# First norms of a decoder block with a state-space layer, taken batch by batch beside the projections, and in part inside the recurrence

## The chip, the cores and the metric

One core of one Trainium2 chip. The time is the device time of one execution in microseconds (us); the time before is the median of 3 runs. TensorE (PE) multiplies matrices, VectorE (DVE), ScalarE (ACT) and GpSimd (POOL) work on tiles of 128 partitions, and SyncE (SP) issues all the DMAs. Each has its own queue, worked off in order; semaphores tie them together.

## The reference, cut to what matters

Four sequences (batches) of 512 positions with 512 features. What the change touches is the front of the first of three layers:

```python
x = x + _L0_attn_ref(_layernorm(x, axis=-1), ...)
# _layernorm: (x - m) / sqrt(v + 1e-5) over the features
# _L0_attn_ref:
res = hidden_states
h = _rmsnorm(hidden_states, rms1_w)       # x * rsqrt(mean(x*x) + 1e-5) * w
h = res + _mamba(h, ...)
# _mamba:
zxbcdt = x @ in_proj_w.T                   # 2688 outputs: z, x, B, C, dt
dt = softplus(dt_in @ dt_proj_w.T + dt_proj_b)
# for each position: h = exp(dt * A) * h + dt * x * B;  y = C * h, summed over 16 states
y = (y + D_skip * x_full) * silu(z)
```

Behind it stand the out projection, an MLP, a quantised attention and an MLP with 4-bit weights; the change leaves them as they are.

## The kernel before

**Layout.** Features lie on the partitions in 4 tiles of 128 (`FT = 4`), positions on the free axis: one batch is 4 x 512 columns, 1 MB. Sums over features are matmuls with a matrix of 1/512 (`mean_w`), whose result is the mean in every partition. The matmuls with data are split: each float is a high part (fp32r) and a low part, and `three_pass` makes three matmuls out of one (high x high, high x low, low x high).

**Norms (on VectorE L1164 to L1201).** All four batches go through each step before the next step begins: x is loaded whole into `xin`; TensorE forms the means (`mean_of`), `centre` subtracts them, ScalarE squares (`norm_squares`), TensorE averages the squares (`squares_mean`), ScalarE takes the root, `rstd` on VectorE the reciprocal, and VectorE writes the normed x into `res`, which SP stores to HBM as `res_d` for use long after. The second norm does the same again with the squares of `res` (`rms_scale`, `split_hi`, `split_lo`), and leaves the high and low parts `xhi` and `xlo`. A barrier of all five engines follows (`phase_end(..., 1)`).

**Lead-in and recurrence.** The loop `for g in range(-2, STEPS)` stands on every engine. A step `g` is one block of 128 of the 1024 channels of one batch (`STEPS = 32`, 8 steps to a batch) and has 16 turns `c`, one for each state. In each turn TensorE spreads a row of dt and one of v over the partitions (`spread_dt`, `spread_v`), ScalarE forms the decay, VectorE multiplies v with B (`make_drive`) and scans along the positions (`scan`), GpSimd multiplies with C (`read_out`), and TensorE gathers (`gather_four`). The rings hold 3 drives, 6 states and 8 read-outs. Steps -2 and -1 are the lead-in: they have no scans and only do the jobs that the first steps need.

A *job* is one of 21 tiles of 128 outputs of the in projection for one batch (`project`), three jobs a step, two steps ahead. Job 0 is dt, 1 is the first tile of x, 2 of B, 3 of C. For batch 0 each needs its weights first: load (`load_wraw`, two buffers), high part on ScalarE (`w_high`), low part on VectorE (`w_low`), and a store of both to `w_d`, from where the other batches load them. ScalarE takes a job's result out of PSUM (`take`), SP spills it to HBM (`spill`), with 4 copies for x and B, and loads it back in the layout that the scan needs (`load_x`, `load_b`, `load_c`). `soft_*` make dt out of job 0, `dt_x` multiplies it with x to v, and `load_pack` copies the high and low halves of dt and v into packs that TensorE spreads from.

**What sets the order.** All orders are written out by hand. SP's queue is in one order too: a load waits behind every wait ahead of it.

## Time and profile before

| | us |
|---|---|
| median of 3 runs | 2953.04 (2950.15 to 2955.85) |
| the profiled execution, its time | 2957.49 |
| its span, first to last instruction | 2955.6 |
| busy: TensorE, VectorE, ScalarE, GpSimd | 2665.8, 2147.2, 1157.1, 1217.0 |
| first scan starts, last scan starts | 146.0, 1108.0 |
| granted TensorE clock, mean over the span | 0.931 |

The profile is of one execution. An instruction's busy time is its own; two neighbours on an engine can overlap a little. Where an engine idles, the profile names what released it. The granted clock is a share of 2.4 GHz: 0.5 is 1.2 GHz. A matmul in plain f32 shows as two rows, each with its own weight load.

### The profile page before, as it was taken

What the parts mean: (1) busy time and instruction counts of PE and PEld (TensorE: products, weight loads), DVE (VectorE), ACT (ScalarE), POOL (GpSimd) and SP (SyncE); (2) the same over time, 40 slices, a digit from 0 to 9 for tenths busy, and PEclk for the clock granted to TensorE, in tenths of its full rate; (3) what the DMA queues carried; (4) which work ended last, traced back from release to release, by engine and by line L of the source; (5) the groups of instructions that cost most, each with busy time, mean ns of one, the idle gap of its engine ahead of it and who ended that gap; (6) DMA issues with size and microseconds to landing.
All of it is one profiled execution on the core that took longest, in us unless ns stands there. A gap on an engine that the chain in (4) does not pass through costs nothing.

```text
span 2955.6 us, 32384 instructions
## 1 busy us (share of the span) xinstructions
PE 2665.8 (90%) x11120; PEld 1892.8 (64%) x11128; DVE 2147.2 (73%) x2711; ACT 1157.1 (39%) x1665; POOL 1217.0 (41%) x816
## 2 busy tenths in 40 slices
PE   6388898889888885699999999999989999999999
PEld 2244344444344424588888877887877788888887
DVE  5499999999999994544346667776867875555553
ACT  3355555555555543432225444343333332222221
POOL 0088898889888870101000104222412422222221
PEclk9699898889899867899999999999999999999999
DMA  3455465464556316412121111212111111111111
GB/s 139 157 170 160 133 178 157 110 201 137 135 164 173 109 50 246 135 44 78 43 72 43 62 39 41 66 43 60 48 42 38 47 46 50 51 48 45 51 50 65
DMA packets 152212, 275.34 MB, mean 93 GB/s; under 512 B 27248, under 2 KB 27760, under 8 KB 151536
## 3 DMA queue, kind: packets, MB, share of 16 engines
q1 hardware_dynamic: 152048, 273.27, 31.1%
q8 instruction: 88, 1.44, 0.2%
q14 instruction: 76, 0.62, 0.1%
HBM read 178.27 MB, written 61.34 MB: 81 GB/s over the span
## 4 chain that ended last, share of the span: by engine, by line
PE 71%; DVE 10%; ACT 8%; issue 5%; POOL 3%; DMA 2%; SPq 1%; DVEq 0%; POOLq 0%; ACTq 0%
PE ps L1596 19%; PE ps L1597 18%; PE ps L1598 18%; PE ps L1636 8%; ACT ps L791 5%; PE ps L1646 4%; DVE state L1255 4%; POOL read L1058 2%; DVE rs L1172 1%; PE ps L1574 1%; DMA vpack<-vl 1%; PE ps L1763 1%; PE ps L1737 1%; PE ps L1707 1%; DMA owraw<-in_out_w 0%
## 5 line engine op out<-in xcount | busy, mean ns | idle before, releaser
L1058 POOL TENSOR_TENSOR read<-state,c_t 128x512 f32<-128x512 f32 x512 | 655.5, 1293 | 142.2 <-DVE state L1255 116.7
L1255 DVE TENSOR_TENSOR_SCAN state<-ps,drive 128x512 f32<-128x512 f32 x512 | 618.4, 1208 | 13.5 <-ACT ps L791 12.4
L1596 PE MATMUL ps<-xh,ghi 128*128 128x512 f32 x1536 | 607.9, 396 | 0.8 <-issue 0.8
L1598 PE MATMUL ps<-xh,glo 128*128 128x512 f32 x1536 | 598.8, 390 | 0.0
L1597 PE MATMUL ps<-xl,ghi 128*128 128x512 f32 x1536 | 598.5, 390 | 0.0
L1105 POOL TENSOR_TENSOR wdeq<-packed,scales 128x1024 f32<-128x1024 f16 x96 | 260.3, 2712 | 798.6 <-DVE packed L1374 798.6
L791 ACT ACTIVATE ps<-ps,a_exp 128x512 f32<-128x512 f32 x512 | 338.9, 662 | 469.0 <-PE ps L1636 467.7
L1541 DVE TENSOR_TENSOR act_o<-act_o,ps 128x512 f32<-128x512 f32 x192 | 131.7, 686 | 313.1 <-PE ps L1598 298.2
L1246 DVE TENSOR_TENSOR drive<-ps,b_t 128x512 f32<-128x512 f32 x512 | 339.8, 664 | 22.6 <-PE ps L1636 22.2
L1636 PE MATMUL ps<-dpack,sel 128*128 128x512 f32 x512 | 260.5, 509 | 104.4 <-DVE state L1255 103.4
L996 ACT ACTIVATE ahi<-act_o 128x512 fp32r<-128x512 f32 x192 | 121.5, 633 | 560.8 <-DVE act_o L1541 560.8
L1596 PEld LDWEIGHTS ps<-xh,ghi 128*128 128x128 f32 x1536 | 288.7, 188 | 63.6 <-issue 4.3
L1597 PEld LDWEIGHTS ps<-xl,ghi 128*128 128x128 f32 x1536 | 288.8, 188 | 61.8 <-issue 3.1
L1598 PEld LDWEIGHTS ps<-xh,glo 128*128 128x128 f32 x1536 | 288.7, 188 | 60.4
L1596 PE MATMUL ps<-ahi,ghi 128*128 128x512 f32 x768 | 306.3, 399 | 20.2 <-issue 20.2
L1597 PE MATMUL ps<-alo,ghi 128*128 128x512 f32 x768 | 300.8, 392 | 0.0
L1598 PE MATMUL ps<-ahi,glo 128*128 128x512 f32 x768 | 300.7, 392 | 0.0
L1636 PE MATMUL ps<-vpack,sel 128*128 128x512 f32 x512 | 251.8, 492 | 36.9 <-DMA vpack<-vl 23.6
L1527 DVE TENSOR_TENSOR res<-res,ps 128x512 f32<-128x512 f32 x192 | 130.8, 685 | 193.0 <-PE ps L1598 190.9
L1636 PEld LDWEIGHTS ps<-dpack,sel 128*128 128x128 f32 x512 | 108.1, 211 | 231.5 <-DVE state L1255 222.0
L1636 PEld LDWEIGHTS ps<-vpack,sel 128*128 128x128 f32 x512 | 106.1, 207 | 229.3 <-issue 97.9
L858 ACT ACTIVATE ghi<-wdeq 128x1024 fp32r<-128x1024 f32 x96 | 100.9, 1051 | 298.1 <-POOL wdeq L1105 266.4
(177 smaller groups left out, 3792.9 us busy)
## 6 DMA issues: line engine op xcount, KB each, us to landing
whi<-w_d SPq DMA_DIRECT2D x63, 256.0 KB, 3.9
wlo<-w_d SPq DMA_DIRECT2D x63, 256.0 KB, 4.8
x_d<-ev SPq DMA_DIRECT2D x32, 256.0 KB, 3.3
x_t<-x_d SPq DMA_DIRECT2D x32, 256.0 KB, 4.8
b_d<-ev SPq DMA_DIRECT2D x32, 256.0 KB
b_t<-b_d SPq DMA_DIRECT2D x32, 256.0 KB, 4.1
c_d<-ev SPq DMA_DIRECT2D x32, 256.0 KB, 3.0
c_t<-c_d SPq DMA_DIRECT2D x32, 256.0 KB, 3.2
```

The lines of the kernel that those rows point to most:

```text
L791: act.activation(ps[:, n % 2, :], ps[:, n % 2, :], ACT.Exp, scale=a_exp[:, col:col + 1]).then_inc(decay_ready, 1)
L996: act.activation(ahi[n // 2][:, cols(n % 2)], act_o[n % 2][:, :], ACT.Copy)\
L1058: pool.tensor_tensor(read[:, n % RRING, :], state[:, n % SRING, :], c_t[:, g % 2, :], ALU.mult).then_inc(read_ready, 1)
L1105: pool.tensor_tensor(wdeq[:, :].rearrange("p (h n) -> p h n", h=2), codes, scale, ALU.mult).then_inc(deq, 1)
L1246: dve.tensor_tensor(drive[:, n % DRING, :], ps[:, 2 + n % 2, :], b_t[:, g % 2, :], ALU.mult).then_inc(drive_ready, 1)
L1255: dve.tensor_tensor_scan(state[:, n % SRING, :], ps[:, n % 2, :], drive[:, n % DRING, :], 0.0, ALU.mult, ALU.add)\
L1527: dve.tensor_tensor(res[:, f, cols(b)], res[:, f, cols(b)], ps[:, free_bank(24 * E + 16 + k), :], ALU.add).then_inc(added, 1)
L1541: dve.tensor_tensor(act_o[n % 2][:, :], act_o[n % 2][:, :], ps[:, free_bank(24 * E + 2 * n + 1), :], ALU.mult)\
L1596: pe.matmul(out_, w_h, x_h, start=(start and k == 0), stop=False)
L1597: pe.matmul(out_, w_h, x_l, start=False, stop=False)
L1598: last = pe.matmul(out_, w_l, x_h, start=False, stop=(stop and k == n - 1))
L1636: pe.matmul(ps[:, bank, :], sel[:, 4 * (j % 2) + m, :], pack[j // 2][:, :], start=True, stop=True).then_inc(done, 1)
```

## The change

- The norms are formed per batch (`column_mean`, `centre`, `squares`, `variance`, one instruction for each of the 4 tiles), in place in `xlr[b]` and `xhr[b]`. Reciprocal roots are two ScalarE instructions, `Ln` and `Exp` with scale -0.5 (`root_1`, `root_2`), so the reciprocals on VectorE go. The mean square of the second norm is worked out from the first (`hat_variance`: variance times the first reciprocal root, twice) and not by squares and matmuls, and `both_roots` multiplies the two reciprocal roots.
- The normed x that is stored to `res_d` (`normalise`) is made by GpSimd: of batches 0 and 1 in the lead-in, of 2 and 3 in steps 2 and 4.
- `scale_x`, `split_hi` and `split_lo` of batch 0 stand in front of its first projection; those of batches 1, 2 and 3 stand in the recurrence, in steps 2 and 3, 10 and 11, 18 and 19.
- The barrier behind the norms goes, and so do two of ScalarE's table loads. The lead-in is written out by hand on each engine in place of steps -2 and -1. The means and variances of batches 1 to 3 stand in it, between the projections.
- Loads of x come batch by batch; batch 0 comes as 4 loads, and the weights of the first two jobs come right behind it.
- `copy_x0` copies the first x tile for step 0 within SBUF instead of through HBM; `load_pack` is cut in two, and for step 0 the packs are loaded ahead of other work. C's tiles 1 and 2 are jobs 4 and 5 (`C_TILES`).

The diff, cut to its core:

```diff
@@ SP
+            for f in range(FT):
+                sp.dma_start(xlr[0][:, f, :], t["x"][:, f, cols(0)]).then_inc(x0_loaded[f], 16)
...
             store_w(0)
             store_w(1)
-            for g in range(-2, STEPS):
+            store_hat(0)
+            store_w(2)
+            copy_x0()
+            load_pack_dt(0)
+            spill(B0)
+            spill(X0)
+            load_pack_v(0)
+            load_b(0)
+            store_w(3)
...
+            for g in range(STEPS):
...
+                if g == 1:
+                    store_hat(1)
+                if g in (4, 6):
+                    store_hat(g // 2)
@@ ACT
+            def root_1(b):
...
+                act.activation(r1, ps[:, VAR_BANK[b], :], ACT.Ln, bias=eps_col[:, 0:1]).then_inc(ln_log, 1)
+                act.wait_ge(ln_log, 2 * b + 1)
+                act.activation(r1, r1, ACT.Exp, scale=-0.5).then_inc(ln_r1, 1)
...
+            squares(0)
+            w_high(0)
+            w_high(1)
+            root_1(0)
...
+            root_2(2)
+            squares(3)
+            take(4)
+            root_1(3)
+            w_high(6)
+            root_2(3)
+            take(5)
+            w_high(7)
...
+                    for b in (1, 2, 3):
+                        if g == CT * b - 5 and c % 4 == 1:
+                            split_hi(b, c // 4)
@@ POOL
+            def normalise(b, f):
+                r1, u = ln_rows[b]
+                pool.wait_ge(ln_r1, b + 1)
+                pool.tensor_tensor(hat(b)[:, f, :], xlr[b][:, f, :], r1, ALU.mult).then_inc(ln_hat, 1)
...
+                    if g in (2, 4) and c % 4 == 3:
+                        normalise(1 + g // 2, c // 4)
@@ DVE
-            def rstd(use, b):
-                dve.wait_ge(root_ready, B * use + b + 1)
-                dve.reciprocal(rs[:, cols(b)], rs[:, cols(b)]).then_inc(rstd_ready, 1)
-                dve.wait_ge(rstd_ready, B * use + b + 1)
...
+                    for b in (1, 2, 3):
+                        if g == CT * b - 6 and c % 4 == 1:
+                            scale_x(b, c // 4)
+                        if g == CT * b - 5 and c % 4 == 2:
+                            split_lo(b, c // 4)
@@ PE
+            pe.wait_ge(mean_loaded, 16)
+            column_mean(0)
+            variance(0)
+            column_mean(1)
+            project_whole(0)
+            project_whole(1)
+            pe.wait_ge(dwlo_ready, 1)
+            dt_project(0)
+            variance(1)
+            project_whole(2)
+            column_mean(2)
+            project_whole(3)
+            dt_project(1)
+            variance(2)
+            column_mean(3)
+            project_whole(4)
+            variance(3)
+            project_whole(5)
```

**The order on TensorE, in front of the first projection.** Rows with `mean_w` are means and mean squares, rows with `whi` or `wlo` the projection. Before, it ended with batch after batch of squares and the barrier:

```order
L1574 MATMUL ps<-sq,mean_w 128x512 x3
L1574 MATMUL ps<-sq,mean_w 128x512 [waits squared]
L1574 MATMUL ps<-sq,mean_w 128x512 x3
L1596 MATMUL ps<-xhi,whi_67 128x512 [waits dwlo_ready,wlo_ready,sel_ready,phase_done]
L1597 MATMUL ps<-xlo,whi_67 128x512
L1598 MATMUL ps<-xhi,wlo_70 128x512
L1596 MATMUL ps<-xhi,whi_67 128x512
```

And now, where batch 0 stands in front of it, and one mean of batch 1:

```order
L1689 MATMUL ps<-xlr_62,mean_w 128x512 [waits x0_loaded3]
L1698 MATMUL ps<-xhr_58,mean_w 128x512 [waits ln_squared] x4
L1689 MATMUL ps<-xlr_63,mean_w 128x512 [waits x_loaded1]
L1689 MATMUL ps<-xlr_63,mean_w 128x512 x3
L1706 MATMUL ps<-xh_50,whi_78 128x512 [waits ln_lo,wlo_ready]
L1707 MATMUL ps<-xl_54,whi_78 128x512
L1708 MATMUL ps<-xh_50,wlo_81 128x512
```

The first projection moved from behind 48 such matmuls and the barrier to behind 12.

**The order on TensorE at the end of the lead-in** (rows with `sel` are the spreads of the recurrence). Before:

```order
L1598 MATMUL ps<-dthi,dwlo 128x512
L1596 MATMUL ps<-xhi,whi_69 128x512
L1597 MATMUL ps<-xlo,whi_69 128x512
L1598 MATMUL ps<-xhi,wlo_72 128x512
L1636 MATMUL ps<-vpack_89,sel 128x512 [waits pack_loaded0]
L1636 MATMUL ps<-vpack_89,sel 128x512
L1636 MATMUL ps<-dpack_85,sel 128x512
```

And now:

```order
L1707 MATMUL ps<-xl_54,whi_79 128x512
L1708 MATMUL ps<-xh_50,wlo_82 128x512
L1698 MATMUL ps<-xhr_61,mean_w 128x512 [waits ln_squared] x4
L1706 MATMUL ps<-xh_50,whi_80 128x512 [waits job_taken,wlo_ready]
L1707 MATMUL ps<-xl_54,whi_80 128x512
...
L1708 MATMUL ps<-xh_50,wlo_83 128x512
L1745 MATMUL ps<-vpack_102,sel 128x512 [waits ln_u,pack_loaded0,ln_centred,sel_ready]
L1745 MATMUL ps<-vpack_102,sel 128x512
L1745 MATMUL ps<-dpack_98,sel 128x512
```

The variance of batch 3 (L1698) now stands between jobs 4 and 5, job 5 is done before the first spread, and that spread waits for the norms' last use of its banks too.

**The order on VectorE in step 2 of the recurrence** (`state` rows are scans, `drive` rows the products in front of them). Before:

```order
L1246 TENSOR_TENSOR drive<-ps,b_t 128x512 [waits scan_done,vb_ready]
L1255 SCALAR_TENSOR_TENSOR state<-ps,drive 128x512 [waits read_ready,decay_ready,drive_ready]
L1246 TENSOR_TENSOR drive<-ps,b_t 128x512 [waits scan_done,vb_ready]
L1255 SCALAR_TENSOR_TENSOR state<-ps,drive 128x512 [waits read_ready,decay_ready,drive_ready]
L1211 TENSOR_TENSOR wlo_72<-wraw,whi_69 128x512 [waits whi_ready]
L1246 TENSOR_TENSOR drive<-ps,b_t 128x512 [waits scan_done,vb_ready]
L1255 SCALAR_TENSOR_TENSOR state<-ps,drive 128x512 [waits read_ready,decay_ready,drive_ready]
```

And now:

```order
L1315 TENSOR_TENSOR drive<-ps,b_t 128x512 [waits scan_done,vb_ready]
L1324 SCALAR_TENSOR_TENSOR state<-ps,drive 128x512 [waits read_ready,decay_ready,drive_ready]
L1279 SCALAR_TENSOR_TENSOR xlr_63<-xlr_63,rms_71,dwraw 128x512 [waits ln_hat,ln_r12]
L1315 TENSOR_TENSOR drive<-ps,b_t 128x512 [waits scan_done,vb_ready]
L1324 SCALAR_TENSOR_TENSOR state<-ps,drive 128x512 [waits read_ready,decay_ready,drive_ready]
L1315 TENSOR_TENSOR drive<-ps,b_t 128x512 [waits scan_done,vb_ready]
L1324 SCALAR_TENSOR_TENSOR state<-ps,drive 128x512 [waits read_ready,decay_ready,drive_ready]
L1290 TENSOR_TENSOR wlo_83<-wraw,whi_80 128x512 [waits whi_ready]
```

A scaling (L1279) stands between a scan and the next drive, four times in this step; in step 3 a low part (L1285) does, and the same for the other two batches in steps 10 and 11, 18 and 19.

## Rows read from the trace of the kernel before

**Rows 1.** Busy us (xcount) by stretch; then clock, DMA share, GB/s.

```profile
0.00:99.00 99.00, 48.06 (x96) 19.80 (x96) 68.02 (x44) 34.03 (x28) 0.20 (x4) 0.81 0.29 103
99.00:146.00 47.00, 26.09 (x84) 20.10 (x85) 8.88 (x11) 15.44 (x26) 6.81 (x5) 0.72 0.73 235
146.00:1108.00 962.00, 833.54 (x3060) 421.60 (x3060) 933.53 (x1100) 501.16 (x814) 841.82 (x665) 0.87 0.51 145
```

**Rows 2.** Scan and drive: ns shortest, median, longest; first and last start.

```profile
L1255 DVE TENSOR_TENSOR_SCAN state<-ps,drive x512: 1200/1207/1224, 146.0 to 1108.0; 128x512 f32<-128x512 f32 x171
...
L1246 DVE TENSOR_TENSOR drive<-ps,b_t x512: 652/661/695, 144.8 to 1106.3; 128x512 f32<-128x512 f32 x171
```

**Rows 3.** Waits on VectorE, 146 to 1108 us: us, times, longest.

```profile
DVE drive L1246 <- PE ps L1636: 14.6, 24, 0.7
DVE state L1255 <- ACT ps L791: 12.4, 31, 0.5
```

**Rows 4.** Groups of instructions, 0 to 99 us: busy us, mean ns, idle before.

```profile
L1172 DVE RECIPROCAL rs<-rs 128x512 f32<-128x512 f32 x8 | 26.8, 3348 | 11.3 <-ACT rs L695 11.2
...
L1186 DVE SCALAR_TENSOR_TENSOR xin<-res,rms,rs 128x512 f32<-128x512 f32 x16 | 11.0, 747 | 0.1
...
L1177 DVE TENSOR_TENSOR xlo<-xin,xhi 128x2048 fp32r<-128x2048 f32 x4 | 9.1, 2286 | 0.0
...
L695 ACT ACTIVATE rs<-ps,eps_col 128x512 f32<-128x512 f32 x8 | 5.0, 684 | 5.5 <-PE ps L1574 5.5
L1211 DVE TENSOR_TENSOR wlo<-wraw,whi 128x512 fp32r<-128x512 f32 x2 | 1.3, 682 | 0.0
```

**Rows 5.** DMA issues, 0 to 4.5 us: KB each, median us to landing.

```profile
xin<-in_x SPq DMA_DIRECT2D x1, 1024.0 KB, 5.9
mean_w<-in_mean_w SPq DMA_DIRECT2D x1, 64.0 KB, 1.8
```

**Rows 6.** Timeline of TensorE, the norms: start us, us.

```profile
26.00 13.90 PE L1574 MATMUL ps<-sq,mean_w 128*128 128x512 f32 x32
44.74 5.40 PE L1574 MATMUL ps<-sq,mean_w 128*128 128x512 f32 x8 [4.85 <-ACT sq L688]
```

**Rows 7.** Timeline of the lead-in.

```profile
114.69 0.64 ACT L762 ACTIVATE sp_exp<-sp_abs 128x512 f32<-128x512 f32 x1
...
115.90 0.62 ACT L775 ACTIVATE sp_log<-sp_exp 128x512 f32<-128x512 f32 x1
116.00 0.69 DVE L1235 SCALAR_TENSOR_TENSOR sp_rest<-ps,sp_exp 128x512 f32<-128x512 f32 x1 [4.97 <-ACT ps L769]
...
117.07 1.63 DVE L1211 TENSOR_TENSOR wlo<-wraw,whi 128x512 fp32r<-128x512 f32 x1 [0.38 <-ACT whi L720]
...
143.51 0.50 PEld L1636 LDWEIGHTS ps<-vpack,sel 128*128 128x128 f32 x2 [16.45 <-DMA vpack<-vl]
```

**Rows 8.** Groups of instructions, 148 to 1300 us.

```profile
L1058 POOL TENSOR_TENSOR read<-state,c_t 128x512 f32<-128x512 f32 x512 | 655.5, 1293 | 142.2 <-DVE state L1255 116.7 <-PE ps L1646 20.4 <-issue 0.5
...
L1211 DVE TENSOR_TENSOR wlo<-wraw,whi 128x512 fp32r<-128x512 f32 x13 | 12.9, 994 | 0.0
```

**Rows 9.** TensorE by stretch: busy us, clock, DMA share, GB/s.

```profile
71.00:99.00 28.00, 0.00 (x0) 0.50 0.00 0
99.00:103.00 4.00, 3.98 (x9) 0.50 0.44 143
...
113.30:119.20 5.90, 5.90 (x27) 0.99 0.71 242
```

**Rows 10.** DMA issues, 99 to 150 us.

```profile
wraw<-in_in_w SPq DMA_DIRECT2D x8, 256.0 KB, 3.9
...
vpack<-vh SPq DMA_DIRECT2D x2, 128.0 KB, 3.9
```

**Rows 11.** The chain that ended last, in the lead-in: start us, us.

```profile
120.03 6.79 DMA b_d<-ev
```

More of the change, by code:

```diff
@@ L79, in build @@
     res = place("res", [P, FT, T], F32, 0)
-    xhi = place("xhi", [P, FT, T], F32R, after())
-    xlo = place("xlo", [P, FT, T], F32R, after())
-    SCAN0 = 32768
-    FREE0 = after()
+    XH0, XL0, FREE0 = 32768, 65536, 98304
+    xh = [place(f"xh{b}", [P, FT, S], F32R, XH0 + 8192 * b) for b in range(B)]
+    xl = [place(f"xl{b}", [P, FT, S], F32R, XL0 + 8192 * b) for b in range(B)]
+    xhr = [place(f"xhr{b}", [P, FT, S], F32, XH0 + 8192 * b) for b in range(B)]
+    xlr = [place(f"xlr{b}", [P, FT, S], F32, XL0 + 8192 * b) for b in range(B)]
     mean_w = place("mean_w", [P, P], F32, (top - base - 3072) // 32 * 32)
@@ L95, in build @@
     round_col = place("round_col", [P, 1], F32, after())
[L98 to L101 removed]
+    NORM_END = FREE0 + 57344
     wraw = place("wraw", [P, 2, FT, P], F32, NORM_END)
@@ L118, in build @@
     dt_t = place("dt_t", [P, S], F32, after())
+    row_r = place("row_r", [P, S], F32, after())
+    row_u = place("row_u", [P, S], F32, after())
     assert after() <= top - base - 3072
@@ L703, in _, with table @@
[L703 to L712 removed]
+            def table(number):
+                act.add_instruction(mybir.InstLoadActFuncSet(
+                    name=nc.get_next_instruction_name(), act_func_set_id=number, ins=[], outs=[]))
@@ L792, in decay, with soften @@
                                scale=a_exp[:, col:col + 1]).then_inc(decay_ready, 1)
+            def soften(q):
+                soft_abs(q)
+                soft_pos(q)
+                soft_exp(q)
+                soft_one(q)
+                soft_log(q)
+            act.wait_ge(consts_ready, 2)
+            table(EXP_LN_SET)
+            squares(0)
+            w_high(0)
+            w_high(1)
+            root_1(0)
+            act.wait_ge(dw_loaded, 16)
+            act.activation(dwhi[:, :], dwraw[:, :], ACT.Copy).then_inc(dwhi_ready, 1)
+            root_2(0)
+            act.wait_ge(loaded_consts, 16 * 6)
+            act.activation(a_exp[:, :], a_log[:, :], ACT.Exp).then_inc(a_ready, 1)
+            for f in range(FT):
+                split_hi(0, f)
+            w_high(2)
+            take(0)
+            squares(1)
+            take(1)
+            soften(0)
+            root_1(1)
+            take(2)
+            w_high(3)
+            dt_high(0)
+            root_2(1)
+            squares(2)
+            v_high(0)
+            w_high(4)
+            take(3)
+            soften(1)
+            root_1(2)
+            w_high(5)
+            root_2(2)
[6 more added lines that the diff above has]
+            w_high(7)
             act.wait_ge(a_ready, 2)
-            act.add_instruction(mybir.InstLoadActFuncSet(
-                name=nc.get_next_instruction_name(), act_func_set_id=EXP_LN_SET, ins=[], outs=[]))
-            for g in range(-2, STEPS):
+            for g in range(STEPS):
                 nb, k, jobs = step_jobs(g)
@@ L1268, in skip_y @@
                                          op0=ALU.mult, op1=ALU.add).then_inc(y_ready, 1)
-            for g in range(-2, STEPS):
+            centre(0)
+            w_low(0)
+            w_low(1)
+            hat_variance(0)
+            dve.wait_ge(dwhi_ready, 1)
+            dve.tensor_tensor(dwlo[:, :], dwraw[:, :], dwhi[:, :].bitcast(F32), ALU.subtract)\
+               .then_inc(dwlo_ready, 1)
+            both_roots(0)
+            dve.wait_ge(loaded_consts, 16 * 6)
+            for f in range(FT + 1):
+                if f < FT:
+                    scale_x(0, f)
+                if f:
+                    split_lo(0, f - 1)
@@ L1271, in _ @@
+            hat_variance(2)
+            w_low(5)
+            centre(3)
+            both_roots(2)
+            hat_variance(3)
+            w_low(6)
+            both_roots(3)
+            w_low(7)
+            dve.tensor_copy(ident16[:, :], ident[:, :]).then_inc(consts_ready, 1)
+            make_drive(0, 0)
+            for g in range(STEPS):
                 nb, k, jobs = step_jobs(g)
                 first = IN_TILES * nb + 3 * k
-                if g == 0:
-                    make_drive(0, 0)
```

371 lines of the change are left out of this document (195 added, 176 removed).

## The prediction, made before the changed kernel was run

> **What bounds the kernel now.** I read the views in this order. First the busy time by stretch [rows 1]: the span falls into a stretch of norms (0 to 99 us), a lead-in (99 to 146), the recurrence (146 to 1108), a gap, and the part behind it, which the change does not touch. In the norms VectorE is busy 68 of 99 us and GpSimd 0.2; TensorE works 48 us of them and the last 28 not at all. In the recurrence VectorE is busy 934 of 962 us. Second, the two instructions that make up the recurrence [rows 2]: 512 scans of 1.21 us and 512 drives of 0.66 us, which is nearly all of the 934. The first scan starts at 146.0 and the last at 1108.0. Third, VectorE's waits in that stretch [rows 3]: 27.0 us in all, none over 0.7. So the recurrence is bound by VectorE, in its own order, and two numbers decide what the change is worth: when the first scan starts, and how much work VectorE does between the first scan and the last.
>
> **What is removed.** The eight reciprocals (26.8 us), the 16 scalings (11.0 us), the batch-wide low parts (9.1 us) and two more batch-wide passes of that length, centring and normalising, all on VectorE [rows 4], stand one behind another in front of the barrier. With them go a second pass of squares on ScalarE and its 16 mean matmuls. The barrier lets the first projection start at 99.0.
>
> **What comes before the first scan now.** Four terms.
>
> (a) *Batch 0 to its first projection.* The first of four 256 KB tiles is issued at about 0.7; before, a 1 MB load took 5.9 us and a 64 KB one 1.8 us [rows 5], so TensorE starts near 4 and is not starved afterwards. A mean or variance block is four matmuls, eight rows in the trace: 13.9 us for 32 of them, so 3.4 us a block at full clock, and 5.4 us for a block begun after idling [rows 6]. Mean ends near 9.7. The first tile's centring (0.6) and square (0.6) run ahead of the rest, so variance ends near 14.5. The two roots need Ln, Exp, two VectorE products, Ln, Exp, one product: with 0.69 us for ScalarE from PSUM [rows 4], 0.61 to 0.64 for Ln and Exp and 0.69 for a dependent VectorE row [rows 7], 4.6 us, and 5.1 with the hand-offs, to 19.7. Eight tile operations on VectorE (four scalings, four low parts), 0.6 each when back to back, and one copy on ScalarE follow: 25.2, and three more passes end projection 0 at 26. The four normalisings move to GpSimd, 1.29 us each [rows 8]; the last ends at 21.4 and is used at about 22.
>
> (b) *TensorE's queue from there.* A projection is 12 passes of 0.23 us at full clock, 2.7 us, or of 0.43 at half, 5.1 (27 passes in 5.9 us and 9 in 4.0) [rows 9]. Projection 1 (2.7) runs while ScalarE copies and VectorE centres batch 1 (2.5), takes a low part (0.6) and splits dt (0.6), so the first dt matmuls end at 29.7. Then in its queue: variance 1, projection 2, mean 2, projection 3, dt, variance 2, mean 3, projection 4, variance 3: five blocks at 3.4, three projections at 2.7 and 0.7 make 25.8, so 55.5.
>
> (c) *Waits inside it.* The raw weights come through two buffers, reloaded by SP after the low part has been stored, 3.9 us to landing [rows 10]. The load of tile 5 now stands on SP behind the packs of step 0, behind eight copies of B and X and behind the load of B, which waits for the copies to land; in the old chain that landing took 6.8 us [rows 11]. ScalarE copies tile 5 before it squares batch 3, so variance 3 is late by it: I take 5 us.
>
> (d) *After variance 3.* Two roots (5.1), the eighth weight tile on ScalarE and VectorE (1.3), two drives (1.3): the first scan at 55.5 + 5 + 7.7 = 68 at full clock. Projection 5 (2.7) and the first spreads lie beside the roots. The packs, loaded 3.9 us after the last half is issued [rows 10], are there by about 51, since SP now issues them ahead of most spills; before, TensorE waited for them until 143.5 [rows 7].
>
> TensorE's clock is the open term. In the old lead-in the granted clock was 0.72 [rows 1]; it was at 1.2 GHz from 99 to 103, after idling, and at 2.4 GHz from 113.3 to 119.2, in a dense run [rows 9]. The new queue is denser than the old one but has waits. At half clock throughout, every block takes 6.8 us and every projection 5.1: (a) and projection 1 end at 38 instead of 29.7, variance 1 to projection 5 are five blocks, four projections and dt once, 34 + 20.5 + 1.3 = 56, and the last step takes some 4: the first scan at 98. I take 5 us more than at full clock, as if 5 us of the work ran at half pace: the **first scan at 73**, between 66 and 98. That is 73 us before the old 146.
>
> The Trainium skill, "TensorE: Matmul & The Clock Gate", Part 1, says that the default state is the throttled one and activity releases it. The row from 71 to 99, idle at 0.50 [rows 9], agrees; the page would not change the sum, only make the half-clock case likelier if waits of (c) are longer than taken.
>
> **What is added to the recurrence.** Batches 1 to 3 are scaled and split there: 12 scalings and 12 low parts on VectorE, all with both inputs in SBUF. The nearest row is the weights' low part, of the same shape, with GpSimd at work beside it: 0.99 us mean of 13 in the recurrence against 0.68 in the norms [rows 4, 8], and once 1.63 [rows 7]. VectorE has no room, so each adds its length less the 0.07 by which neighbours overlap: 24 x 0.92 = **22 us**, between 24 x 0.58 = 14 and 24 x 1.56 = 37. They do not wait: hats and roots of each batch are a step or more older. ScalarE gets 12 copies of 0.6, with 461 of 962 us free; no cost. GpSimd gets eight normalisings, 10.3 us, in steps 2 and 4. A step is 16 read-outs and 5 others, 27 us of its time in about 32 that such a step takes VectorE; 5.2 more makes 32. Six state buffers cover a lag, so nothing, at most 2 us a step. SP stores 1 MB of hats at steps 1, 4 and 6; DMA is busy 0.51 there [rows 1] and the next step's loads have a step of slack: nothing. If that cover went, three times 3 us. TensorE loses nothing; its projections read other tiles of the same size.
>
> By a rule of the Trainium skill the price would be higher. "SBUF — State Buffer", § Who interferes with whom, says that VectorE with two SBUF inputs and GpSimd reading SBUF exclude each other for a whole instruction. Here an addition could wait out a read-out of 1.29 us: 24 x (0.68 + 1.29 - 0.07) = 45 us instead of 22. The 13 low parts, at 0.99 on average, say that most of the wait does not fall on VectorE, and I keep 22; the 45 is a rival below.
>
> **Sum.** 73 saved, 22 given back: 51 us. The profiled execution took 2957.5 (span 2955.6); 2957.5 - 51 = 2906.5. It stood 4.45 above the median of 2953.04, so against the median **2902**.
>
> **Rivals.**
>
> *Clock and waits (17%).* TensorE stays mostly at half clock, or waits on each hand-off; the first scan is at 98. For it: the 0.72. Against: full clock in every dense stretch. 2953 - 48 + 22 = 2927.
>
> *All overlaps (12%).* First scan at 67, and the additions cost 14 or fill some of the 27.0 us of VectorE's waits: 2953 - 79 + 14 = 2888.
>
> *Whole-instruction exclusion (7%).* As worked out from the two lengths: 2953 - 73 + 45 = 2925.
>
> *The norms of batch 0 don't start the work sooner (2%).* All first loads share one queue. If the tile that projection 2 needs lands only after some 6 MB are in, about 20 us later than taken, the first scan is at 93: 2922. Against: the loads before drained by 21, and the first weight copies here stand ahead of 3 MB of x.
>
> *Lock-step (2%), the other side.* The place is TensorE's in-order queue: each mean and variance of batches 1 to 3 stands in front of a projection and waits for centring and squares. If nothing overlaps, a batch costs mean 6.8, centring 2.5, square 0.6, variance 6.8 and roots 5.1, 22 us, and the lead-in keeps its 47: 26 + 47 + 66 = 139. With the additions at 37 us: 2953 - 7 + 37 = 2983. It decides once the first scan is later than 146 - 22 = 124. Against it: the order puts a projection or a block of another batch between nearly all links.
>
> **How the numbers follow.** My forecast, 2902, has 60%; its own terms give 2890 to 2915. A measurement of this kernel can tell about 0.2%, 6 us, from no change. Four cases of five lie more than 6 us below 2953, and only lock-step is above; with it, and a little for its milder forms, faster is 97%, same 1%, slower 2%. The range 2884 to 2928 takes in the clock, overlap and exclusion cases at their centres and leaves out their tails and lock-step.
>
> **What would show it.** The first projection near 22 and the first scan near 73 (66 to 98); granted clock in the stretch from 20 to 73 above 0.8; TensorE there busy well over half; the distance from first to last scan 962 + 22 = 984, with scalings and low parts in it at 0.9 to 1.0 us; the 1847.6 us from the start of the last scan to the end of the span unchanged. The forecast is wrong if the first scan is later than 98, if the additions exceed 1.6 us each, or if steps 2 and 4 grow by more than their own VectorE work, which would be GpSimd.

## The result, and the profile after

| | before | after |
|---|---|---|
| median, measured together (4 runs each) | 2953.70 us | 2904.87 us (2903.83 to 2910.90) |
| ratio | | 0.984, 95% interval 0.9828 to 0.9852 |
| the profiled execution, its time and span | 2957.49, 2955.6 | 2910.90, 2909.1 |
| first scan, last scan | 146.0, 1108.0 | 78.4, 1059.7 |
| from first to last scan | 962.0 | 981.3 |
| from the start of the last scan to the end of the span | 1847.6 | 1849.4 |
| granted TensorE clock, mean | 0.931 | 0.939 |

The kernel is 1.6% faster; 2902 was predicted, with a range of 2884 to 2928. In the profiled execution, the first scan comes 67.6 us earlier, the distance to the last is 19.3 us longer and the part behind 1.8 longer: 67.6 - 19.3 - 1.8 = 46.5, which is the difference of the two spans.

The busy time by stretch, which answers to [rows 1] (columns: TensorE, its weight loads, VectorE, ScalarE, GpSimd, then clock, DMA share and GB/s):

```profile
0.00:26.00 26.00, 13.94 (x26) 5.76 (x27) 13.27 (x17) 9.90 (x16) 7.02 (x8) 0.93 0.91 314
26.00:74.00 48.00, 39.35 (x119) 24.01 (x118) 22.29 (x34) 26.73 (x46) 12.29 (x9) 0.86 0.55 175
74.00:1056.00 982.00, 837.25 (x3056) 419.91 (x3054) 955.42 (x1126) 508.29 (x828) 858.79 (x671) 0.87 0.51 147
```

Norms and lead-in are now one stretch in which TensorE is busy 53 of 74 us. Taken exactly from the first scan to the last, VectorE is busy 955.6 of 981.3 us, against 933.5 of 962.0 before: 22.1 us more work and 2.8 us less idle time make the 19.3 by which the distance grew. GpSimd went from 842 to 861.

The scan, as in [rows 2], and VectorE's waits from the first scan on, as in [rows 3]:

```profile
L1324 DVE TENSOR_TENSOR_SCAN state<-ps,drive x512: 1198/1216/1231, 78.4 to 1059.7; 128x512 f32<-128x512 f32 x171
```

```profile
DVE state L1324 <- ACT ps L827: 11.6, 27, 0.8
DVE drive L1315 <- PE ps L1745: 11.2, 18, 0.7
```

The waits of these two lines fell by 4.2 us (27.0 to 22.8), all idle time together by 2.8, so the work that was added took little of them. Its own price, in the groups of instructions from 90 to 1060 us (busy us, mean ns):

```profile
L1290 DVE TENSOR_TENSOR wlo<-wraw,whi 128x512 fp32r<-128x512 f32 x12 | 12.0, 1000 | 0.0
L1285 DVE TENSOR_TENSOR xl<-xlr,xh 128x512 fp32r<-128x512 f32 x12 | 11.9, 991 | 0.0
L1279 DVE SCALAR_TENSOR_TENSOR xlr<-xlr,rms,selraw 128x512 f32<-128x512 f32 x4 | 4.4, 1104 | 0.0
L1279 DVE SCALAR_TENSOR_TENSOR xlr<-xlr,rms,row_u 128x512 f32<-128x512 f32 x4 | 4.1, 1028 | 0.0
L1279 DVE SCALAR_TENSOR_TENSOR xlr<-xlr,rms,dwraw 128x512 f32<-128x512 f32 x4 | 3.4, 862 | 0.0
```

The low parts of the weights stayed where they had been (994 ns in [rows 8], 1000 now), and the low parts of x cost the same. The 24 added instructions are busy 23.8 us. Less 0.07 each where neighbours overlap that makes 22.1. How much of the distance they cost is known to about 4 us only, since a distance is read from one execution: it grew by 19.3 against the kernel before (962.0), but the run with Ln and Exp alone, further down, has the same recurrence as the kernel before and a distance of 958.2, from which it would be 23.1.

TensorE's timeline in front of the first scan (start us, us, then in brackets the idle time before and what ended it):

```profile
3.68 6.18 PE L1689 MATMUL ps<-xlr,mean_w 128*128 128x512 f32 x8 [3.68 <-DMA mean_w<-in_mean_w]
11.30 3.70 PE L1698 MATMUL ps<-xhr,mean_w 128*128 128x512 f32 x8 [1.44 <-ACT xhr L730]
14.84 3.60 PE L1689 MATMUL ps<-xlr,mean_w 128*128 128x512 f32 x8
25.37 0.77 PE L1706 MATMUL ps<-xh,whi 128*128 128x512 f32 x1 [6.93 <-DVE xl L1285]
...
33.41 3.60 PE L1698 MATMUL ps<-xhr,mean_w 128*128 128x512 f32 x8
...
55.83 0.39 PE L1708 MATMUL ps<-xh,wlo 128*128 128x512 f32 x1
64.87 6.30 PE L1698 MATMUL ps<-xhr,mean_w 128*128 128x512 f32 x8 [8.65 <-ACT xhr L730]
```

There are two holes, 6.93 us in front of the first projection and 8.65 us in front of batch 3's variance, and the block behind the second takes 6.30 us instead of 3.60. The granted clock was 0.98 in the hole from 57 to 60, 0.50 from 61.5 to 64.8, 0.58 over this block and 1.00 behind it. The chain that ended last shows what the second hole is (start us, us, what):

```profile
42.96 0.46 SPq L523
...
43.46 1.72 SPq L524
...
45.23 0.71 SPq L502
...
50.14 1.75 SPq L502
...
51.93 0.51 SPq L502
...
52.48 1.09 SPq L502
...
57.53 0.43 SPq L470
...
58.00 4.17 DMA wraw<-in_in_w
...
62.20 0.64 ACT whi L761
...
62.86 0.69 DVE wlo L1290
63.55 0.61 DVE xlr L1259
...
64.19 0.64 ACT xhr L730
...
64.87 6.32 PE ps L1698 x8
```

`L502` is the line that spills B and X: eight copies, between 45.23 and 53.57, that SyncE issues one after another at about 1 us each. The store of weight tile 3, with which the load of tile 5 is issued, stands behind them. From 42.96 to 58.00 this chain is SyncE's issuing alone, 14.3 us without a wait; of the 21.9 us up to the start of the variance no other engine or transfer has as much.

### The profile page after: what moved, and what is told of

Same layout as the page of the kernel before. It is cut to its first block, busy times and chain, and to the rows that moved or that the text cites. A ratio compares the mean times of both kernels' runs of the same rounds, so it can differ in the third digit from the quotient of the medians.

```text
span 2909.1 us, 32439 instructions
## 1 busy us (share of the span) xinstructions
PE 2651.7 (91%) x11096; PEld 1882.2 (65%) x11096; DVE 2135.0 (73%) x2735; ACT 1153.9 (40%) x1690; POOL 1247.4 (43%) x832
## 4 chain that ended last, share of the span: by engine, by line
PE 72%; DVE 10%; ACT 8%; issue 4%; POOL 3%; DMA 1%; SPq 1%; DVEq 0%; POOLq 0%; ACTq 0%
PE ps L1706 19%; PE ps L1707 19%; PE ps L1708 19%; PE ps L1745 8%; DVE state L1324 5%; ACT ps L827 5%; PE ps L1757 5%; POOL read L1140 2%; PE ps L1897 1%; PE ps L1871 1%; PE ps L1841 1%; DMA vpack<-vl 0%; DVE drive L1315 0%; DVE act_o L1650 0%; DMA owraw<-in_out_w 0%
## 5 line engine op out<-in xcount | busy, mean ns | idle before, releaser
L1140 POOL TENSOR_TENSOR read<-state,c_t 128x512 f32<-128x512 f32 x512 | 665.3, 1311 | 144.9 <-DVE state L1324 126.7
L1324 DVE TENSOR_TENSOR_SCAN state<-ps,drive 128x512 f32<-128x512 f32 x512 | 622.8, 1217 | 13.8 <-ACT ps L827 11.6
L1315 DVE TENSOR_TENSOR drive<-ps,b_t 128x512 f32<-128x512 f32 x512 | 344.4, 673 | 11.9 <-PE ps L1745 11.2
```

What stands on the lines that cost most here:

```text
L1140: pool.tensor_tensor(read[:, n % RRING, :], state[:, n % SRING, :], c_t[:, g % 2, :], ALU.mult).then_inc(read_ready, 1)
L1315: dve.tensor_tensor(drive[:, n % DRING, :], ps[:, 2 + n % 2, :], b_t[:, g % 2, :], ALU.mult).then_inc(drive_ready, 1)
L1324: dve.tensor_tensor_scan(state[:, n % SRING, :], ps[:, n % 2, :], drive[:, n % DRING, :], 0.0, ALU.mult, ALU.add)\
```

## The experiments

All stand against the kernel before, measured with them (its medians 2954.22 to 2955.03; 2953.70 beside the change). "First scan" and "distance" are of the profiled execution, and distances of kernels with the same recurrence differ by up to 2 us among the changed ones and by 3.8 between the kernel before and that with Ln and Exp. The intervals of neighbours in this table overlap; where a difference of 4 or 5 us is called one below, the single executions of the two kernels don't overlap. The changed kernel's own profile was its slowest execution; in three experiments that leave the lead-in's critical path alone (24 more products, scalings early, late turns), the first scan stood at 76.7, 76.8 and 77.5, so 77 is its usual place.

| kernel | median us | ratio (95%) | first scan | distance |
|---|---|---|---|---|
| change | 2904.87 | 0.9828 to 0.9852 | 78.4 | 981.3 |
| load of tile 5 first | 2900.96 | 0.9800 to 0.9832 | 72.4 | 981.8 |
| filler | 2905.13 | 0.9817 to 0.9848 | 75.6 | 980.0 |
| norms first | 2932.25 | 0.9908 to 0.9941 | 103.4 | 981.0 |
| before, with Ln and Exp | 2937.86 | 0.9925 to 0.9955 | 128.7 | 958.2 |
| 24 more products | 2918.26 | 0.9862 to 0.9895 | 76.7 | 992.9 |
| late turns | 2907.18 | 0.9824 to 0.9853 | 77.5 | 981.8 |
| scalings early | 2899.75 | 0.9795 to 0.9831 | 76.8 | 976.3 |
| SyncE order 1 | 2901.50 | 0.9804 to 0.9834 | 72.0 | 980.8 |
| SyncE order 2 | 2897.67 | 0.9793 to 0.9820 | 68.9 | 980.1 |
| all together | 2898.13 | 0.9797 to 0.9824 | 67.9 | 978.3 |
| order 2, six scalings in idle time | 2892.51 | 0.9781 to 0.9808 | 68.7 | 973.9 |

In all eleven experiments the stretch behind the last scan was 1844.4 to 1848.7 us. It is unchanged within 4 us, and what moves the time beyond that are the two numbers the prediction had named.

### What the lead-in waits for

**The load of weight tile 5 moved ahead of the copies.**

```diff
             load_pack_dt(0)
+            store_w(3)
             spill(B0)
...
             load_b(0)
-            store_w(3)
```

> Theory: in the changed kernel the first scan (78.4 us) is set by SP's queue: the load of weight tile 5 is issued at 58.0 behind eight copies of B and X, and variance 3 and both roots of batch 3 follow it. Here SP stores tile 3 and loads tile 5 ahead of these copies, all else as it was. Variance 3 should begin near 57 instead of 64.9 and the first scan come 5 to 9 us earlier, 70 to 73; loads of tiles 6 and 7 are late next. Median near 2898. Rival, TensorE's own work sets the lead-in: nothing moves, 78. Rival, the packs and B for step 0 set it: they are issued 1.4 us later here, so the first scan comes later, 79 to 80.

Median 2900.96, 3.9 below the change; the first scan 6.0 earlier in the profile. Its TensorE timeline and its chain of waits:

```profile
56.73 3.70 PE L1698 MATMUL ps<-xhr,mean_w 128*128 128x512 f32 x8
```

```profile
58.38 4.02 DMA c_d<-ev
...
64.20 5.58 DMA wraw<-in_in_w
```

The hole of 8.65 us and the slow block are gone, at one line moved: the cause is shown. Not all of the 11 us between 64.87 + 6.30 and 56.73 + 3.70 reach the first scan, for another thing is late next: the load of tile 7, which stands behind the wait for the spill of C on the same queue. TensorE now has a hole of 5.65 us later, in front of a spread. The first scan came where the theory had it; the median was 3 us above its 2898.

**A filler in the hole**, to tell the wait from the clock: 36 matmuls whose result is not used, which leave the wait as it is.

```diff
             project_whole(4)
+            for k in range(36):
+                pe.matmul(ps[:, 0, :], xh[0][:, 0, 0:P], xh[0][:, 0, :], start=True, stop=True)
             variance(3)
```

> 36 matmuls whose result nobody reads stand between job 4 and variance 3, where TensorE waits 8.7 us and its granted clock falls to 0.50. Theory: the clock stays at full, variance 3 takes 3.4 us instead of 6.3, and the first scan comes 2.9 us earlier, 75.5; median near 2902. Rival, the granted clock isn't what makes variance 3 long or what follows waits for something else: 78.4 as before, or later by what the 36 overrun.

```profile
64.75 3.62 PE L1698 MATMUL ps<-xhr,mean_w 128*128 128x512 f32 x8
```

The block starts where it did, and takes 3.62 us instead of 6.30: behind a hole of 8.65 us TensorE was at 1.2 GHz for most of it (0.58), behind matmuls at 2.4 (1.00). The first scan came 2.8 us earlier in the profile (1.4 against the usual 77), but the median, 2905.13, is the change's, where 2902 had been expected. The clock alone is worth less here than can be told; the hole is what costs.

**The norms of batches 1 to 3 put ahead of the first projection**, to see what the order by itself is worth. Kept are Ln and Exp, the tile-by-tile passes, the missing barrier.

```diff
             pe.wait_ge(mean_loaded, 16)
-            column_mean(0)
-            variance(0)
-            column_mean(1)
+            for b in range(B):
+                column_mean(b)
+                variance(b)
             project_whole(0)
```

(and the same on ScalarE and VectorE.)

> The changed kernel with all means, variances and roots of batches 1 to 3 in front of the first projection instead of between the projections; nothing is removed. Theory: TensorE's six blocks (20.6 us at full clock) and the root chains then delay the first projection from 25.4 to about 46, and the lead-in behind it needs some 40 instead of 53, so the first scan comes at 84 to 92, 6 to 14 us later, median 2911 to 2919: the order between the projections is worth about a third of these norms' cost. Rival, the order is worth their whole cost: the first scan at 100 or later. Rival, SP's queue sets the lead-in so far that it makes no difference: 78 to 80.

Median 2932.25, 27.4 above the change, first scan at 103.4: the theory's 84 to 92 failed, and the rival with 100 or later held. VectorE's timeline:

```profile
31.04 0.69 DVE L1261 TENSOR_TENSOR dwraw<-dwraw,ps 128x512 f32<-128x512 f32 x1 [5.58 <-ACT dwraw L741]
...
41.09 0.69 DVE L1261 TENSOR_TENSOR selraw<-selraw,ps 128x512 f32<-128x512 f32 x1 [4.10 <-ACT selraw L741]
...
51.08 0.69 DVE L1261 TENSOR_TENSOR row_u<-row_r,ps 128x512 f32<-128x512 f32 x1 [4.04 <-ACT row_r L741]
```

The same step of three batches is 10.0 us apart. Mean, centring, square, variance and roots of a batch are one chain through three engines, and with nothing between them nothing fills its gaps. In the change they are filled with projections. This is the lock-step rival in a mild form: 10 us a batch, not 22, since the next batch's mean still lies beside the roots.

**The kernel before, with its eight reciprocals replaced by Ln and Exp.**

```diff
-                    act.activation(rs[:, cols(b)], bank, ACT.Sqrt, bias=eps_col[:, 0:1])\
+                    act.activation(rs[:, cols(b)], bank, ACT.Ln, bias=eps_col[:, 0:1])\
...
+                    act.activation(rs[:, cols(b)], rs[:, cols(b)], ACT.Exp, scale=-0.5)\
...
+            act.add_instruction(mybir.InstLoadActFuncSet(
+                name=nc.get_next_instruction_name(), act_func_set_id=EXP_LN_SET, ins=[], outs=[]))
...
-                dve.reciprocal(rs[:, cols(b)], rs[:, cols(b)]).then_inc(rstd_ready, 1)
```

> The kernel before with one part of the change alone: the eight reciprocal roots are Ln and Exp on ScalarE, the eight reciprocals of 3.35 us on VectorE are gone, everything else stays, the barrier and the batch-wide order too. Theory: VectorE's chain in front of the barrier loses 26.8 us less what ScalarE's second instruction and the next wait give back, so the first scan comes 20 to 27 us earlier than 146, near 123, and the median is near 2930; the order and the barrier are worth the rest of the 68 us. Rival, the reciprocals are the whole of it and the order nothing: 2905. Rival, the squares and mean matmuls take over as the bound: less than 15 us gained.

First scan 17.3 us earlier, median 2937.86, 16.9 below the kernel before: between what the theory (20 to 27) and the rival (less than 15) had said. Two of ScalarE's four table loads up to the lead-in, 1.28 us each, went with the square roots. VectorE's groups from 0 to 82 us, in the two passes that use the roots:

```profile
L1189 DVE SCALAR_TENSOR_TENSOR xin<-res,rms,rs 128x512 f32<-128x512 f32 x16 | 10.9, 748 | 11.6 <-ACT rs L698 11.5
...
L1202 DVE TENSOR_TENSOR res<-xin,rs 128x2048 f32<-128x2048 f32 x4 | 8.9, 2288 | 7.8 <-ACT rs L698 7.8
```

VectorE lost the 26.8 us of [rows 4] and waits 19.3 us for roots instead of 11.2; 26.8 less these 8.1 is 18.7, near the 17.3 by which the first scan moved. Of the 68 us by which the first scan moved, some 17 belong to the roots with their table loads and some 25 to the order; the two were measured from different kernels and need not add up. What the barrier, the missing second pass of squares and the early packs make of the rest was not tried apart.

### What the additions to the recurrence cost

**24 more of them.** Subtractions of the same shape, from SBUF to SBUF, with a result that nobody uses, in steps 12 to 14.

```diff
+                    if g in (12, 13, 14) and c % 2 == 0:
+                        dve.tensor_tensor(flat(wraw[:, 0, :, :]), xh[0][:, 0, :].bitcast(F32),
+                                          xl[0][:, 0, :].bitcast(F32), ALU.subtract)
```

> 24 more subtractions on VectorE of the kind that the change put into the recurrence (128x512, both inputs in SBUF, the result into a buffer nobody reads), in steps 12 to 14. Theory of the prediction, 0.92 us each in a stretch that VectorE fills: the distance from the first to the last scan grows by 22 us, from 981.3 to 1003, and the median to 2927. Rival, VectorE has slack and part of them is free: under 14. Rival, each waits out a whole GpSimd instruction: 45.

The median rose by 13.4 us, the distance by 11.6. The theory's 22 failed, and the number is that of the first rival, under 14; but slack was not the reason. Over the steps in which they stand, from one skip product (`y_t`) to the fifth after it, the time went from 148.5 to 164.1 us, 0.65 us each, which is their busy time, 0.717, less the overlap of 0.07. The other 4 us by which the distance is shorter lie in steps that are the same in both kernels. In the groups of instructions from 455 to 560 us, first of the change, then of this kernel:

```profile
L1140 POOL TENSOR_TENSOR read<-state,c_t 128x512 f32<-128x512 f32 x57 | 72.9, 1290 | 13.0 <-DVE state L1324 12.6
```

```profile
L1140 POOL TENSOR_TENSOR read<-state,c_t 128x512 f32<-128x512 f32 x50 | 72.0, 1450 | 15.4 <-DVE state L1324 15.2
...
L1392 DVE TENSOR_TENSOR wraw<-xh,xl 128x512 f32<-128x512 f32 x24 | 17.2, 717 | 0.0
```

The added instruction took 717 ns, hardly more than alone, and GpSimd's read-outs went from 1290 to 1450 ns. Somebody does wait, but here it is GpSimd, which has time. In the change it is VectorE in part (0.99 us). So what an addition costs is its own length in both cases, and it is the length that differs. What decides which of the two engines waits was not settled; the next run tried one idea.

**The scalings and low parts in turns 10 to 13 of their steps instead of one in every four turns** (and ScalarE's high parts in turns 8 to 11).

```diff
-                        if g == CT * b - 6 and c % 4 == 1:
-                            scale_x(b, c // 4)
-                        if g == CT * b - 5 and c % 4 == 2:
-                            split_lo(b, c // 4)
+                        if g == CT * b - 6 and 10 <= c < 14:
+                            scale_x(b, c - 10)
+                        if g == CT * b - 5 and 10 <= c < 14:
+                            split_lo(b, c - 10)
```

> The scalings and low parts of batches 1 to 3 stand in turns 10 to 13 of their steps, one a turn, instead of in every fourth turn from 1 and 2. Theory: what one costs depends on whether GpSimd reads at that moment; turns 0, 1, 2, 6 and 8 have a second GpSimd instruction, turns 9 to 15 have one and idle time. In turns like that 24 more cost 0.5 us each, here 24 cost 0.84. So the steps with them get shorter by 24 x 0.3 = 4 to 8 us in all, first to last scan near 975, median near 2898. Rival, the place in a step doesn't matter: 981. Rival, four in a row pile up behind GpSimd or the states' ring: longer, 985.

Median 2907.18, distance 981.8: no gain, as the first rival had it. The same groups as above, of this kernel:

```profile
L1290 DVE TENSOR_TENSOR wlo<-wraw,whi 128x512 fp32r<-128x512 f32 x12 | 14.3, 1193 | 0.0
L1285 DVE TENSOR_TENSOR xl<-xlr,xh 128x512 fp32r<-128x512 f32 x12 | 10.7, 893 | 0.0
```

The low parts of x became 98 ns cheaper and the scalings some 150, those of the weights 193 ns dearer; the 36 together are busy 35.1 us instead of 35.8. The place in the step moves most of the wait from one instruction to another and does not remove it.

**The scalings of batches 1 and 2 in the lead-in**, with the normalising of batch 2, which must be first.

```diff
             hat_variance(2)
+            for f in range(FT):
+                scale_x(1, f)
             w_low(5)
...
             both_roots(2)
+            for f in range(FT):
+                scale_x(2, f)
...
-                        if g == CT * b - 6 and c % 4 == 1:
+                        if b == 3 and g == CT * b - 6 and c % 4 == 1:
```

> The scalings of batches 1 and 2 and the hats of batch 2 move from the recurrence into the lead-in, where VectorE stands idle from 54 to 63 and from 66.5 to 72.6 and GpSimd from 53.6 to 79.8. Theory: there they are free, and the distance from first to last scan falls by 8 x 0.9 = 7 us, the first scan stays at 78.4 within 1 us; median near 2898. Rival, the place in the recurrence is as good since VectorE waits there anyway (27 us in all): the distance falls by less than 3 us. Rival, they delay centring 3 or the roots: the first scan comes up to 5 us later.

Median 2899.75, 5.1 below the change; the distance fell by 5.0 where 7 had been expected, the first scan did not move from its usual place. Eight instructions in time that VectorE idled away cost nothing, and 0.63 us each came back.

### Is there a better kernel

**SyncE's queue in another order**, twice. The first put the weight tiles forward, and X and C behind tile 4 and B's load:

```diff
             load_pack_dt(0)
+            store_w(3)
             spill(B0)
-            spill(X0)
             load_pack_v(0)
             load_b(0)
-            store_w(3)
-            spill(3)
             store_w(4)
+            spill(X0)
+            spill(3)
+            store_w(5)
             load_c(0)
             load_x(1)
-            store_w(5)
```

> SP's queue in the lead-in in another order: tile 3 stored and tile 5 loaded ahead of the copies of B, the packs of v and B's load ahead of the copies of X, tiles 4 and 5 stored ahead of the store of C. In the run with tile 5 first alone the first scan came at 72.4 and then waited for tile 7, whose load stood behind the wait for C. Theory: SP's order is the bound and this one frees more of it: first scan at 67 to 69, median 2895. Rival, the copies themselves (8.8 us of issuing) only move, and their late landing holds up tile 4's result or step 1's x: 72 or later.

Median 2901.50, no better than moving tile 5 alone: the rival held. B's load now stands close behind B's copies and waits for them to land, and the X copies, pushed back, land late themselves:

```profile
48.64 7.51 DMA b_d<-ev
...
60.05 4.15 DMA x_d<-ev
```

The second left the X copies behind the B copies and moved weight tile 3 ahead of both, and tiles 4 and 5 ahead of the spill of C:

```diff
             load_pack_dt(0)
+            store_w(3)
             spill(B0)
             spill(X0)
             load_pack_v(0)
             load_b(0)
-            store_w(3)
-            spill(3)
             store_w(4)
+            store_w(5)
+            spill(3)
             load_c(0)
             load_x(1)
-            store_w(5)
```

> SP's queue alone, in a third order: tile 3 stored and tile 5 loaded ahead of the copies of B and X, both sets of copies where they were, then the packs of v and B's load, then tiles 4 and 5 stored (and 6 and 7 loaded) ahead of the store of C and its wait. The run with tile 5 first alone was held up by tile 7 behind the wait for C (72.4), the run with X's copies late by their landing (72.0). Theory: each order shows the next wait on SP, and with both out of the way variance 3, ending near 60, and its roots are next: first scan 67 to 70, median near 2896. Rival: the copies' issuing, 8.8 us, keeps the packs until 61, and the first scan stays at 72.

Median 2897.67, 7.2 below the change; first scan 68.9, as the theory had it.

**All of it together**: order 2, the scalings early, job 5 ahead of batch 3's variance, and batch 3's roots and weight tile 7 moved into step 0.

```diff
             project_whole(4)
-            variance(3)
             project_whole(5)
+            variance(3)
...
             centre(3)
             both_roots(2)
-            hat_variance(3)
+            for f in range(FT):
+                scale_x(1, f)
             w_low(6)
-            both_roots(3)
-            w_low(7)
+            for f in range(FT):
+                scale_x(2, f)
...
+                    if g == 0 and c == 1:
+                        w_low(7)
+                    if g == 0 and c == 4:
+                        hat_variance(3)
+                    if g == 0 and c == 7:
+                        both_roots(3)
```

> The pieces that gained, together: the third SP order; scalings of batches 1 and 2 and hats of batch 2 in the lead-in; project 5 ahead of variance 3; the roots of batch 3 and weight tile 7 in the turns of step 0. Theory: the first scan then waits for the packs, B and the sixth projection only, 64 to 67, and the distance from first to last scan is 981 - 5 for the scalings + 3 for the products and the tile that move in, near 979: median 2886 to 2891, faster than both kernels. Rival: the gains overlap, since the lead-in's idle time that the scalings use is the time that the SP order takes away: the first scan at 70 or later, median 2896 or more.

Median 2898.13, the same as order 2 alone, where 2886 to 2891 had been expected. Its chain:

```profile
58.50 4.15 DMA wraw<-in_in_w
...
62.67 0.64 ACT whi L761
...
64.61 2.07 DVE xlr L1284 x3
...
66.81 1.20 DVE drive L1320 x2
```

The scalings of batch 2 (L1284) stand behind the low part of tile 6, for which VectorE waits, and in front of the first drive: 2.7 us of them are on the path. What had been taken out of the lead-in went to step 0, where VectorE is full: the distance, 978.3, is 2.0 longer than with the scalings early alone.

**Order 2 with six of the eight scalings put where VectorE idles**: four in the 3.5 us in front of batch 3's first products, two in the 1.6 us in front of tile 6's low part; batch 2 is normalised in the lead-in again, and nothing is moved into step 0.

```diff
             both_roots(2)
+            for f in range(FT):
+                scale_x(1, f)
             hat_variance(3)
+            scale_x(2, 0)
+            scale_x(2, 1)
             w_low(6)
             both_roots(3)
```

> SyncE's second order with six of the eight scalings of batches 1 and 2 put into VectorE's idle time of that lead-in (3.5 us in front of batch 3's first products, 1.6 us in front of weight tile 6's low part), the last two of batch 2 left in step 10, and batch 2 normalised behind batch 1 on GpSimd in the lead-in. Theory (an added instruction costs its length wherever VectorE is full and nothing where it idles on the first scan's path): first scan stays near 69, the distance from first to last scan falls from 980.1 by 6 x 0.84 = 5 to 975, median 2893, 4.5 below 2897.7. Rival (the lead-in is as full as it looks after e_best: what is put there delays the first scan by as much): first scan 72 to 74, distance 975, median 2897 to 2898.

Median 2892.51 (2889.76 to 2895.13, none as slow as the fastest of order 2, 2896.89), ratio 0.9795. First scan 68.7, distance 973.9; 69, 975 and 2893 had been expected. Its VectorE timeline:

```profile
59.11 3.75 DVE L1281 SCALAR_TENSOR_TENSOR xlr<-xlr,rms,dwraw 128x512 f32<-128x512 f32 x4
62.78 0.68 DVE L1268 TENSOR_TENSOR row_u<-row_r,ps 128x512 f32<-128x512 f32 x1
63.49 0.69 DVE L1270 TENSOR_TENSOR row_u<-row_u,row_r 128x512 f32<-128x512 f32 x1
64.11 1.41 DVE L1281 SCALAR_TENSOR_TENSOR xlr<-xlr,rms,selraw 128x512 f32<-128x512 f32 x2
65.43 0.68 DVE L1292 TENSOR_TENSOR wlo<-wraw,whi 128x512 fp32r<-128x512 f32 x1
```

No row has an idle time before it, and the first scan did not move. This is the best kernel of the study: 62.5 us below the one before, against 48.8 for the change.

## Why the prediction was right, point by point

**What bounds it.** Right. The part behind the last scan stayed within 1844.4 to 1849.4 us in every kernel that was run, so first scan and distance account for the rest. The other signs that had been named came too: from 20 to 73 us the granted clock was 0.84 and TensorE busy 39 of 53 us.

**(a) Batch 0 to its first projection.** 22 predicted, 25.37 measured. Mean and variance were sized right (the variance ended at 15.0, 14.5 was said). The step that was too short is the roots, which were through at 22.2 instead of 19.7: GpSimd's four normalisings stand beside them (16.47 to 23.3, 1.7 us each instead of 1.29), and of VectorE's three products there the second and third took 1.15 and 1.75 us where 0.69 had been taken for each; the low part of dt's weights, 2.28 us, stands between them, which the sum had left out. The first scaling, beside the last normalising, took 1.57 us instead of 0.6. The first nine passes also ran at half clock behind the 6.93 us hole (0.50 from 25.4 to 29.2), so that projection 0 was through at 30 rather than 26. Together variance 1 began 3.7 us late, at 33.4 instead of 29.7.

**(b) TensorE's queue.** 22.4 us predicted from variance 1 to the end of projection 4; from 33.41 to 56.2 it took 22.8. Full clock, no waits, as said.

**(c) The wait for tile 5.** Right in place and cause, too small: 5 predicted, 8.65 measured. SyncE never waited for the copies to land; the eight issues themselves took 8.3 us of its time, and the packs behind them 2.7. The prediction had counted the copies as things to be waited for and given their issue no price of its own; its 5 us was taken without a working.

**(d) After variance 3.** 7.7 predicted, 7.3 measured (71.2 to 78.5).

**Clock.** 5 us was taken for the half-clock share, without a working. Of it 2.9 went to the block behind the hole (6.30 instead of the 3.4 taken for a block), which the filler took back; what the first projection lost is counted in (a). Against the 68 at full clock the errors are 3.7 + 0.4 + 3.7 + 2.9 - 0.4 = 10.3, which gives 78.3; measured 78.4 (77 is the usual place), predicted 73.

**Additions.** 22 predicted, 19.3 measured. The three pairs of steps that hold them grew by 6.4, 6.7 and 7.0 us from skip product to skip product, 20.1 in all or 0.84 each, against 0.92 taken. Measured from the run with Ln and Exp alone they grew by 7.0, 8.0 and 7.0, 22.0 in all or 0.92 each. So the term was right within what one execution tells. The first pair, which also holds GpSimd's normalising of batch 2, grew no more than the others; steps 4 and 5, with that of batch 3, grew 0.6 each (0.2 and nothing from the run with Ln and Exp). So GpSimd's additions cost nearly nothing, as said, though its read-outs became about 1% longer (1293 in [rows 8] to 1308 ns from 148 to 1300 us).

**The rivals.** Half clock throughout fell: 0.86 from 26 to 74 us. Whole-instruction exclusion would have asked for 45 us. The Trainium skill, "SBUF — State Buffer", § Who interferes with whom, says that the shared port is an exclusive lock and that the order of issue decides who blocks. The runs agree that one waits, and that either can be the one (0.99 instead of 0.68 us on VectorE; 1450 instead of 1290 ns on GpSimd); a full wait for every addition they do not show, since VectorE's rows are 0.3 us longer on average and the longest low part of x, 1.65 us, is 1.0 longer. The late start fell too: projection 2 began at 36.44 without a wait for its tile. So did the case in which all overlaps: the first scan was later than 67 and the additions took more than 14 us. Lock-step fell, by the order: the run with the norms first shows that it was the real danger, at 27 us.

The two errors in the profiled executions, 5 us on the first scan (4 from its usual place) and 3 on the distance, have opposite signs; the median came out 3 us from the forecast partly for that, which is luck. Inside the first number luck has a part too: the 5 us for the clock, of which the block took 2.9, covered a part of what (a) and (c) were short of.

## What to carry to other kernels

Count each DMA of a moved step as time of the queue that issues it, before asking when it lands: a load behind eight issues made the longest idle time of TensorE in this lead-in, 8.65 us. When chains through several engines must share a stretch, put other work between their links; the order alone was worth 27 us here. Work that has to be added to an engine that is full belongs into that engine's idle time just in front, but instruction by instruction into gaps of a known length: six instructions so placed gained 5 us, while eight, four of them behind the wrong wait, gained nothing in a kernel that also moved work into a full step.

## What was not expected of the hardware

Issuing a DMA is not a constant: in the chain above SyncE took from 0.43 us (a weight store, `L470`) to 1.75 us (a copy of B or X, `L502`) for one, 1.00 on average for the eight copies, and the load of a pack (`L524`) took 1.72 once. What lengthens it was not tried. An instruction added to a full VectorE, with both inputs in SBUF, cost its own length less the overlap: 0.65 us at a busy time of 0.717 (24 more, in their steps), 0.84 to 0.92 at 0.99 (the change). The length is what varies beside GpSimd, and where it stayed short GpSimd's read-outs grew from 1290 to 1450 ns: there the conflict was paid by the engine with time to spare. And a block of eight matmul rows behind a hole of 8.65 us took 6.30 us, mostly at 1.2 GHz, against 3.62 behind filler matmuls at 2.4, of which the median showed nothing.
